# Attention row maxima by key tile with VectorE's transposing maximum; narrow sums of exponentials on GpSimd

## The reference

```python
scores = jnp.einsum('bqhd,bkhd->bhqk', q_full, k_full) * softmax_scale
causal = jnp.tril(jnp.ones((S, S), dtype=bool))
scores = jnp.where(causal[None, None], scores, jnp.finfo(scores.dtype).min)
attn = jax.nn.softmax(scores, axis=-1)
out = jnp.einsum('bhqk,bkhd->bqhd', attn, v).reshape(B, S, H * VD)
```

## Time and profile before

| | |
|---|---|
| median of 3 runs | 752.55 us (752.33 to 752.96) |
| the profiled execution | span 751.0 us from first to last instruction; its whole time is not given apart from it, so what lies around the span is taken as 1.55 us, the distance to the median |
| busy | PE 719.2 us (96%), DVE 541.3 (72%), ACT 326.3 (43%), POOL 207.5 (28%) |
| granted PE clock | 0.999 of full over the span |
| opening maxima | 52.7 to 85.6 us |
| windows 0 to 6 | about 84.5 to 467.8 us |
| window 7, output and feed-forward | the rest |

### The profile page before, as it was taken

How to read it: one execution, slowest core, us unless ns; L and a number is a source line. 1 busy time by engine, 2 the same in 40 slices (tenths; PEclk the granted TensorE clock), 3 DMA queues, 4 the chain that set the end, 5 groups by cost and what they waited for, 6 DMA issues and landing times.

```text
span 751.0 us, 10449 instructions
## 1 busy us (share of the span) xinstructions
PE 719.2 (96%) x3829; PEld 502.7 (67%) x3829; DVE 541.3 (72%) x802; ACT 326.3 (43%) x499; POOL 207.5 (28%) x197
## 2 busy tenths in 40 slices
PE   2889999999999999999999999999999999999997
PEld 1756566666666666666666666555788888887886
DVE  6878689799799799799799889686893323213432
ACT  4844545545545545554554444444254322222210
POOL 1149534144144144144144020100463000000211
PEclk9999999999999999999999999999999999999999
DMA  8934633403403403403403580440210422200101
GB/s 319 257 84 111 142 76 85 103 1 85 103 0 85 103 1 85 103 1 84 104 2 83 123 327 2 168 168 1 84 29 1 127 84 63 58 10 1 42 30 43
DMA packets 40211, 63.43 MB, mean 84 GB/s; under 512 B 4512, under 2 KB 20896, under 8 KB 38304
## 3 DMA queue, kind: packets, MB, share of 16 engines
q1 hardware_dynamic: 40160, 62.75, 30.6%
HBM read 32.99 MB, written 2.10 MB: 47 GB/s over the span
## 4 chain that ended last, share of the span: by engine, by line
PE 72%; DVE 22%; issue 3%; ACT 1%; DMA 1%; SPq 0%; DVEq 0%; ACTq 0%
PE PS L987 16%; PE PS L811 8%; PE PS L1004 8%; PE PS L892 7%; PE PS L874 7%; PE PS L881 6%; PE PS L877 6%; DVE PR L1539 5%; PE PS L951 5%; DVE NMa L1449 4%; PE PS L802 4%; DVE wide L1539 3%; PE PS L824 2%; DVE NMd L1454 2%; DVE NMb L1449 1%
## 5 line engine op out<-in xcount | busy, mean ns | idle before, releaser
L1199 ACT ACTIVATE PR<-PS 128x1024 f32<-128x1024 f32 (+1 forms) x144 | 133.1, 929 | 149.1 <-PE PS L881 118.0
L811 PE MATMUL PS<-KH,Q 96*128 96x128 f32 (+3 forms) x576 | 131.2, 330 | 6.2 <-DVE NMa L1449 4.8
L1449 DVE TENSOR_REDUCE NMa<-PS 128x1 f32<-128x512 f32 (+3 forms) x184 | 117.7, 657 | 25.0 <-PE PS L811 22.8
L811 PEld LDWEIGHTS PS<-KH,Q 96*128 96x128 f32 x576 | 86.7, 190 | 60.9 <-issue 32.4
L874 PE MATMUL PS<-Q,KH 96*128 96x512 f32 x288 | 118.6, 412 | 0.0
L1539 DVE TENSOR_TENSOR PR<-PR 128x2048 f32<-128x2048 f32 (+3 forms) x56 | 112.8, 2014 | 3.6 <-ACT PR L1199 1.2
L881 PE MATMUL PS<-Q,KH 97*128 97x512 f32 (+1 forms) x288 | 114.2, 397 | 0.2 <-DMA Q<-NM 0.2
L877 PE MATMUL PS<-Q,KL 96*128 96x512 f32 (+1 forms) x288 | 113.6, 394 | 0.0
L1787 POOL TENSOR_SCALAR_AFFINE_SELECT diag<-diag 128x512 f32<-128x512 f32 x64 | 47.3, 739 | 195.9 <-ACT diag L1142 195.7
L874 PEld LDWEIGHTS PS<-Q,KH 96*128 96x128 f32 x288 | 54.6, 189 | 27.8 <-issue 14.3
L892 PE MATMUL PS<-PR,V 128*32 128x512 f32 (+3 forms) x704 | 70.2, 486 | 0.0
(11 more groups left out here) (192 smaller groups left out, 1066.9 us busy)
## 6 DMA issues: line engine op xcount, KB each, us to landing
Q<-TQ SPq DMA_DIRECT2D x56, 384.0 KB, 6.2
RT<-in_wo SPq DMA_DIRECT2D x4, 1024.0 KB, 4.8
TQ<-in_wo SPq DMA_DIRECT2D x4, 1024.0 KB, 5.1
Q<-TQ SPq DMA_DIRECT2D x16, 192.0 KB, 3.4
WI<-in_gate_w SPq DMA_DIRECT2D x10, 256.0 KB, 3.5
WI<-in_up_w SPq DMA_DIRECT2D x10, 256.0 KB, 3.9
DI<-in_down_w SPq DMA_DIRECT2D x10, 256.0 KB, 2.7
PR<-in_wmod_c SPq DMA_DIRECT2D x2, 1024.0 KB, 6.5
```

What stands on the lines that cost most here:

```text
L811: ins = pe.matmul(bank[:, i * w:(i + 1) * w], M.Q[0:KR, g % 2, 0, qt // 4, h0 + i, qs], M.KH[0:KR, lo:lo + w], start=(i == 0), stop=(i == ...
L1199: act.activation(tiles, banks, ACT.Exp).then_inc(S_.p, 1)
L1449: dve.tensor_reduce(dst, PS[:, bank_of(turn), 0:n * w].rearrange("p (h k) -> p h k", k=w), axis=AX.X, op=ALU.max, negate=True).then_inc(S_ ...
```

## The change

1. **Parts by key tile.** `PARTS` becomes the 36 pairs (query tile, key tile at or behind it). Each is one matmul of 512 columns: the key tile is stationary, the query tile of all 4 heads moves. A bank holds 128 keys x (4 heads x 128 queries).
2. **Transposing maximum.** DVE reduces each bank with `apply_transpose=True`: in every 32 x 32 block the partitions become the free axis, so 128 keys x 512 queries become 4 blocks of keys x 16 values on each partition, kept in `MX`. There is no other read of a bank: ACT's copy, POOL's select and DVE's second reduce of the diagonal parts are gone.
3. **Mask by contraction rows.** The diagonal parts use all 128 rows of `KH` and of the high `Q`, whose mask rows now hide later keys in that product alone (`mask_rows` has other numbers). The three products of the scores keep their form.
4. **Join.** Two DVE reduces over the key tiles (512 values for queries 0 to 511, 1024 for the rest), then PE's turn, then a DVE reduce over the four blocks of keys straight into `NM` (before, an ACT copy). `NM` is 128 x 32 instead of 32 x 128, so the DMA has 128 pieces of 128 bytes.
5. **Narrow adds on POOL.** The adds of steps 256 and 128 wide, four in a window, run on POOL (`narrow_add`); the order through `ad` stays.
6. **Planner.** Parts cost 0.7 each and are spread evenly, `join` 1.2; narrow adds cost DVE nothing. In a middle window this gives: parts 33 and 34 in u28, part 35 and `join` in u29, `rows` in u31 (no values ahead of it there); the second "odd" goes to u18 (before u20), right behind "even" in u17 and in the same bank.
7. **SP.** The copy of the high mask rows to the second `Q` buffer is sent in the opening, ahead of the queries of group 1, the low one where both were.

```diff
-PARTS = maxima_parts()
+PARTS = [(qt, kt) for qt in range(NS) for kt in range(qt + 1)]
...
+def add_is_narrow(s):
+
+    return width(s) <= 2 * P
...
+    places = [(begin + (end - begin) * k / len(PARTS), ("part", k), 0.7) for k in range(len(PARTS))]
+    return places + [(end + 0.02, ("join",), 1.2), (end + 0.12, ("rows",), 0.3)]
...
     def maxima_part(g, k):
-        qt, lo, w, h0, n = PARTS[k]
+        qt, kt = PARTS[k]
+        f, rows = qt // 4, P if is_diagonal(k) else KR
         bank = side_bank(TURN[("part", g, k)])
...
+        pe.matmul(bank, M.KH[0:rows, kt * P:(kt + 1) * P], M.Q[0:rows, g % 2, 0, f, :, qt % 4 * P:(qt % 4 + 1) * P],
+                  start=True, stop=True).then_inc(S_.side, 1)
...
     def part_reduced(g, k):
...
+        dve.tensor_reduce(M.MX[:, kt, qt // 4, :, qt % 4, :],
+                          PS[:, bank_of(turn), :].rearrange("p (h s q) -> p h s q", h=HG, q=L), axis=AX.X, op=ALU.max,
+                          apply_transpose=True).then_inc(S_.free[bank_of(turn) - FIRST_BANK], 1)
...
     def join(g):
 
+        last = ("part", g, len(PARTS) - 1)
+        dve.wait_ge(S_.free[bank_of(TURN[last]) - FIRST_BANK], freed(last))
         if g > 0:
             dve.wait_ge(S_.side, TURN[("rows", g - 1)] + 1)
+        for f in range(2):
+            dve.tensor_reduce(M.NMj[:, f].rearrange("p h n s -> p (h n s)"),
+                              M.MX[:, 0:NS // 2 * (f + 1), f].rearrange("p k h n s -> p (h n s) k"), axis=AX.X,
+                              op=ALU.max).then_inc(S_.nm, 1)
+
+    def rows_reduced(g):
+        turn = TURN[("rows", g)]
+        dve.wait_ge(S_.side, turn + 1)
+        if g > 0:
+            dve.wait_ge(S_.nd, 16 * g)
+        dve.tensor_reduce(M.NM[:], PS[:, bank_of(turn), 0:P].rearrange("p (k q) -> p q k", q=L), axis=AX.X, op=ALU.max,
+                          negate=True).then_inc(S_.free[bank_of(turn) - FIRST_BANK], 1)
...
+    def narrow_add(w, s):
+
+        qb, kt = STEPS[s]
+        wd = width(s)
+        j = ADDS.index(s)
+        pool.wait_ge(S_.p, NEXP * w + LAST_EXP[s] + 1)
+        pool.wait_ge(S_.ad, NADD * w + j)
+        sums = M.SUM[qb][:, :, QB - wd:QB]
+        pool.tensor_tensor(sums, sums, M.slot(s)[:, :, 0:wd], ALU.add).then_inc(S_.ad, 1)
```

More of the change, by code:

```diff
@@ L40 @@
 COLUMN_PARTS, ROW_PARTS = [1, 0, 4, 3], [2, 5]
[L43 to L59, removed]
-PARTS = maxima_parts()
+PARTS = [(qt, kt) for qt in range(NS) for kt in range(qt + 1)]
 HANDED = (1,)
 def is_diagonal(k):
-    return PARTS[k][1] == PARTS[k][0] * P
+    return PARTS[k][0] == PARTS[k][1]
 def mask_levels():
-    sizes = [2] * (MASK_ROWS * 2 - 3) + [3] * 3
+    sizes = [4] * (MASK_ROWS - 3) + [5] * 3
     starts = [sum(sizes[:n]) for n in range(len(sizes))]
@@ L143 @@
 LATE_SUMS = [s for n in range(NUNIT) for ago, s in SUMS[n] if ago]
+WIDE_ADDS = [s for s in ADDS if not add_is_narrow(s)]
+NARROW_ADDS = [s for s in ADDS if add_is_narrow(s)]
 def blocks_of(qb):
@@ L670, in sp_program @@
         if w == 0:
-            sp.wait_ge(S_.pj, NS)
             sp.wait_ge(S_.nd, 16)
-            for hl in range(2):
-                copy_mask_rows(hl, S_.mq)
+            copy_mask_rows(1)
         if w < G - 2:
@@ L872, in scores @@
             if w == 1:
-                pe.wait_ge(S_.mq, 32)
+                for hl in range(2):
+                    pe.wait_ge(S_.mq[hl], 16)
         pe.matmul(dst, M.KH[0:KR, ks], M.Q[0:KR, w % 2, 0, qb, :, qs], start=True, stop=False)
@@ L903, in pe_program @@
         if st == 0:
[L904 removed]
+            pe.wait_ge(S_.mask, 3)
             keep_busy(7, 3)
@@ L1121, in latent_high @@
         act.activation(M.TQ[:, 2, 0, cols], PS[:, bank_of(turn), :], ACT.Copy).then_inc(S_.lh, 1)
-    def rows_copied(g):
-        turn = TURN[("rows", g)]
-        act.wait_ge(S_.side, turn + 1)
-        if g > 0:
-            act.wait_ge(S_.nd, 16 * g)
-        act.activation(M.NM[:], PS[0:HG * NS, bank_of(turn), 0:P], ACT.Copy).then_inc(S_.free[bank_of(turn) - FIRST_BANK], 1)
     def gate_copied(key):
@@ L1163, in side @@
             gate_copied(key)
-        elif key[0] == "rows":
-            rows_copied(key[1])
         elif key[0] == "split":
             split_high(key[1], key[2])
-        elif key[0] == "part" and is_diagonal(key[2]):
-            diagonal_copied(key[1], key[2])
         elif key[0] == "high":
@@ L1511, in side @@
             latent(g, key[2])
-        elif kind == "part" and not is_diagonal(key[2]):
+        elif kind == "part":
             part_reduced(g, key[2])
-        elif kind == "least":
-            diagonal_reduced(g, key[2])
+        elif kind == "rows":
+            rows_reduced(g)
         elif kind == "join":
@@ L1806, in side @@
             weights_low(g)
-        elif kind == "part" and is_diagonal(key[2]):
-            diagonal(g, key[2])
         elif kind == "even" and g in HANDED:
@@ L1832, in pool_program @@
         for n in range(NUNIT):
+            for ago, s in SUMS[n]:
+                if ago <= w and s in NARROW_ADDS:
+                    narrow_add(w - ago, s)
             for name in TABLES[w][n]:
                 side(name)
+    for s in LATE_SUMS:
+        if s in NARROW_ADDS:
+            narrow_add(G - 1, s)
     normalise(G - 1, 1)
```

134 lines of the change are left out of this document (48 added, 86 removed).

## The result

| | before | after |
|---|---|---|
| median | 752.52 us (752.33 to 752.96, 4 executions) | 764.65 us (761.56 to 767.05, 4 executions) |
| ratio | | 1.0157, 95% interval 1.0131 to 1.0183 |
| profiled execution | span 751.0 | 767.05, span 765.3, mean granted clock 0.983 |

The kernel is slower by 12.1 us, twice the forecast of 5.7 and within its range. The four executions after lie 5.5 us apart, and they line up with the granted clock: 761.56 at 0.993, 763.84 at 0.991, 765.47 at 0.987, 767.05 at 0.983. Before, four executions lie within 0.63 us.

What follows compares the result with a forecast made beforehand. PE sets the pace, with DVE trailing closely enough to hold it up. Second parts +13.2, first parts -5.2, window 6 -0.8 and opening -1.5 sum to +5.7 us: 758 us, range 742 to 769.

Steps and rivals of the forecast that it cites:

- the second part's: Window from u16 to the next u0: PE waits 2.4 us for DVE's join; 32.5 us in all, +2.2 us.
- turn to next u0: End of a window: 4.9 us instead of 3.09, since a unit and the values of (1,4) now follow the turn.
- first part: Window from u0 to u16: cheaper parts reach den 0.6 us earlier, waits for DVE eat some; -0.8 us, window 0 -1.2.
- den's turn to join end on DVE: DVE's stretch in the second part: 24.05 us becomes 24.75; the prediction falls if over 1.5 us off.
- The opening's turn: Opening, DVE-bound: DVE loses only holes between 53 and 73 us, POOL eight selects, PE 2.34 us; taken as -1.5 us.
- Window 6: Window with the join but neither rotations nor odd: +0.2 us in the second part, -1.0 in the first, -0.8 in all.
- The adds on POOL: Narrow adds, 7.4 us a window on POOL: nobody waits, cost 0 with a cover of 2.5 us.
- such a meeting: POOL's rotation and norm meeting DVE's add of (1,2), one waiting for the other's end; ±1 us a window.
- rival 1: DVE keeps up, stretch to the join's end under 22.5 us: 734 us, or 743 with half the holes; chance 0.29.
- the maximum takes one pass: Against the rival of two passes, 1.24 us each: 865 us; at 0.75 to 0.8, 790; chance 0.09 together.
- no change: Rival: the holes eat exactly what PE gains, DVE 1 us a window better than walked; 752.5 us, chance 0.11.
- the maxima landed late: Rival: the 0.7 us cover is gone, PE idles at each window's start, 1 us x 7 more; 765 us, chance 0.08.

Runs made afterwards that it cites:

- the join by tile, planned: Changed kernel with the maxima joined per query tile in eight small reduces, the planner counting 0.2 each and moving the second odd and the join; 758.33 us.
- the last version: Changed kernel with later turn, maxima joined per query tile, parts spread to 0.72 of the window, and odd banks, lat and low later; 745.25 us.
- The join by tile: Changed kernel with later turn and maxima joined per query tile in eight reduces, early pieces costed at nothing so other places stay; 747.41 us.

## Why the prediction was right in direction and wrong in size

**The step that failed** is the second part's: "it waits 2.4 us", priced as 2.4 us. The wait was there and was 2.25 us. But the price of a hole in PE was taken as its length. At five of the six, PE ran on at half its clock, which added 1.5 to 2.9 us each in the profiled execution and 7.6 to 8.0 us in the medians. With the hole filled the kernel takes 757.03 us, 4.2 more than the kernel before beside it; the forecast was 758, 5.7 more. The rows of before could not give this size, since the largest hole there is 1.10 us in the windows and their opening, and its clock is 0.999 over the span; but the text named a hole twice as long as any in those rows and did not ask what the clock does at it.

**What held**, in the undisturbed window from 133.38 to 190.55:

| term | forecast | measured |
|---|---|---|
| turn to next u0 | 4.9 | 138.40 - 133.38 = 5.02 |
| first part | 25.0 | 163.42 - 138.40 = 25.02 |
| u16 to turn | 27.65 | 190.55 - 163.42 = 27.13 |
| den's turn to join end on DVE | 24.75 | 190.40 - 166.19 = 24.2 |
| join, from its start to its end | 1.8 | 1.51 |
| wait ahead of the turn | 2.4 | 2.25 |
| wait at the second odd | 1.2 | 0.87 |
| maximum in a full queue | 0.62 | 0.60 |

PE's busy time fell by 719.2 - 701.3 = 17.9 us in the version with the later turn (2.24 us a group, forecast 2.34). A middle window lost 1.0 us, not 1.4. The opening's turn, at 82.47 before, came at 81.72, 82.02 and 82.20 in three versions with the same opening: 0.3 to 0.8 us earlier, not 1.5, with a wait of 1.44 us ahead of it.

Window 6 was read too short: 467.00 in the earlier trace rows is not its end. Most of the last three units and a block of values are still to come there, and u0 of window 7 starts at 469.77:

```profile
469.77 0.50 PE L874 MATMUL PS<-Q,KH 96*128 96x512 f32 x1
```

From its u0 to that one window 6 took 50.85 us before and 49.26 with the holes filled: -1.6, forecast -0.8. With the clock whole the terms add up: window 0 +1.1, windows 1 to 5 +1.0 each, window 6 -1.6, the opening -0.4, in all +4.1 us of span (755.1 against 751.0). That this lies near the forecast of +5.7 is in part luck, since five middle windows priced 0.4 too high each and a window 6 priced 0.8 too high stand against an opening priced 1.1 too low. The hole stands in six windows, not in the seven that the text named: PE did not wait for the join in window 6.

**The adds on POOL** were costed at nothing, with a cover of 2.5 us, and no row shows PE or DVE held by them in the changed kernel. What the text got wrong there is the other side: it said that they stand "where DVE has time". Leaving them on DVE costs the new kernel 7.6 to 8.7 us, 1.3 us or more in each middle window's first part. POOL's rotation got longer (its mean is 2241 ns, it was 1433) without a wait of PE's that names it; the moved adds are not the reason, since with them on DVE the mean is 2386 to 2396. The one at 172.69 took 3.20 us and began while DVE was in a wide add (172.47 to 174.74). The Trainium skill (SBUF — State Buffer, the shared port pair) calls the pair of ports that DVE and POOL share an exclusive lock, held for the whole instruction; DVE's add of 2.96 us at 184.08 above, beside one of 2.28 at 190.32, fits that: it began while POOL was in a subtraction.

```profile
182.47 2.42 POOL L1761 TENSOR_TENSOR TQ<-RT,TQ 128x1024 fp32r<-128x1024 f32 x1 [4.09 <-ACT TQ L1114]
```

The forecast had counted on such a meeting as ±1 us a window; it came out at 0.7 for this add and 0.4 for that of 177.81, beside POOL's norm of 177.10, and is in the 24.2 us of the stretch.

**The rivals.** DVE did not keep up (its stretch was 24.2 us, over the 22.5 at which rival 1 decides); the maximum takes one pass, as far as 689 ns against 678 show it; the time moved clear of no change; the maxima landed late (0.2 to 0.8 us in a middle window) only in versions with the turn later.

**What the change's parts are worth**, each run set against the kernel before beside it: maxima by key tile with two large reduces and the later turn, 760.43 - 753.05 = +7.4 us; POOL's adds on top, -7.6; the turn where the change put it, +4.4 as a wait and +8.0 as clock, together the +12.1 but for rounding. The join by tile, with the later turn, is worth -5.1.

## What to carry to other kernels

Where a change makes a new hole in TensorE, price what runs behind it too: here 2.2 us of idle cost up to 3 us more at half clock, and either a few matmuls of no use or a consumer placed one unit later took that away. Judge a move of work between engines with the order of all other work held still, since a planner that recounts moves banks and hides the effect. Work taken off an engine that the bounding one waits for is worth more after a change that fills it: the same four adds were worth 2.8 us, and then 7.6 and 8.7.

## What the runs showed of the hardware

- With holes of 2.17 us (the kernel before with the earlier turn) the granted clock went to 0.5 in six windows of six, with holes of 2.25 us (the changed kernel) in five of six, in one profiled execution each. Where it fell inside the hole (all six of the first, two of the second) it stayed there for about 6.8 us and cost 2.9 to 3.0 us; where it fell up to 1 us after TensorE had gone on (three of the second) it stayed for about 3.4 us and cost 1.5 to 1.6. Behind a hole of 1.23 us in window 6 it fell in one profiled execution (the join by tile, planned) and not in the others that have it; at holes of 1.24 us in six windows of that same execution it did not, nor at 1.44 us in the opening or at 1.61 us in the opening of the last version. So a hole's length alone doesn't tell; a long one made a fall likely, and what decides the rest is open. No run has a hole between 1.61 and 2.17 us. The Trainium skill (TensorE: Matmul & The Clock Gate, Part 1) describes the lower state as the default that activity releases; the runs with the filled hole agree, at 0.999.
- The changed kernel, with such holes, scatters: 761.56 to 767.05 us, against 756.86 to 757.37 with the holes filled.
- A maximum over a transposed 128 x 512 block costs DVE 689 ns, the plain one 678.
- POOL's add of 1024 values takes 2376 to 2486 ns, DVE's 1225.
